# Attention output kept channel-major in a fused transformer-block kernel

## The reference

```python
x = L0_attn_x                       # (8, 1024, 256) float32
xn = layernorm(x)
q, k, v = split(xn @ W_attn + b_attn)      # 16 heads of 16 channels
q, k = rope(q), rope(k)                    # rotated by head index
att = softmax(causal(q @ k.T / 4))
s = (att @ v) @ W_proj + b_proj
h = silu(xn @ w_gate.T / 127) * (xn @ w_up.T / 127)      # hidden size 768
g = silu(h @ w_down.T / 127)
return x + s * g
```

## Time and profile before

| what | value |
|---|---|
| median of 3 runs | 1252.62 us (1247.04 to 1253.52) |
| the profiled execution's own time | 1248.4 us |
| its span, first to last instruction | 1246.7 us |
| mean granted TensorE clock | 0.992 |
| VectorE, ScalarE, GpSimd busy | 85%, 75%, 56% |

### The profile page before, as it was taken

The page is one execution under the profiler, slowest core; times in us unless marked ns, Lnnn a source line. Parts: engine busy times, 40 slices in busy tenths (PEclk is TensorE's granted clock), DMA queues, the critical chain, the costliest instruction groups (busy, mean ns, idle before and its releaser), DMA issues.

```text
span 1246.7 us, 28514 instructions
## 1 busy us (share of the span) xinstructions
PE 1180.0 (95%) x10044; PEld 507.0 (41%) x10044; DVE 1062.2 (85%) x3250; ACT 934.1 (75%) x1736; POOL 692.0 (56%) x858
## 2 busy tenths in 40 slices
...
DMA packets 55923, 73.10 MB, mean 59 GB/s; under 512 B 8382, under 2 KB 34372, under 8 KB 55780
## 3 DMA queue, kind: packets, MB, share of 16 engines
...
## 4 chain that ended last, share of the span: by engine, by line
PE 61%; DVE 18%; POOL 8%; ACT 7%; issue 5%; SPq 1%; DMA 1%; POOLq 0%; DVEq 0%; ACTq 0%
PE ring L838 28%; PE acc L829 13%; PE st L778 9%; PE ring L805 6%; DVE ring L1198 5%; DVE mx_a L1202 4%; ACT pexp L1037 2%; PE ring L911 2%; POOL hf L1526 2%; DVE ln L1233 1%; DVE ga L1266 1%; PE ring L947 1%; POOL hT L1535 1%; ACT yT L1044 1%; DVE ynT L1279 1%
## 5 line engine op out<-in xcount | busy, mean ns | idle before, releaser
L1037 ACT ACTIVATE pexp<-st 128x512 f32<-128x512 f32 x1152 | 623.3, 598 | 124.1 <-PE st L778 121.0
L1198 DVE CUSTOM_DVE_ANT_0 ring<-ring,tri 128x512 f32<-128x512 f32 (+3 forms) x1024 | 470.3, 523 | 29.3 <-PE ring L805 28.9
L1496 POOL TENSOR_SCALAR_AFFINE_SELECT pexp<-pexp 128x512 f32<-128x512 f32 x256 | 157.9, 635 | 407.1 <-ACT pexp L1037 407.1
L1202 DVE TENSOR_REDUCE mx_a<-ring 128x1 f32<-128x512 f32 x512 | 328.4, 684 | 17.1 <-PE ring L805 14.6
L829 PE MATMUL acc<-pexp,v_pad 128*17 128x512 f32 (+3 forms) x3072 | 303.7, 490 | 3.0 <-POOL pexp L1496 0.9
L805 PE MATMUL ring<-k_st,q_st 56*128 56x512 f16 (+4 forms) x1536 | 243.9, 326 | 14.9 <-POOL k_st L1617 3.7
L778 PE MATMUL st<-q_st,k_st 58*128 58x512 f16 (+3 forms) x1536 | 234.4, 331 | 6.3 <-ACT pexp L1037 3.8
L778 PEld LDWEIGHTS st<-q_st,k_st 58*128 58x128 f16 x1536 | 62.2, 93 | 267.8 <-ACT pexp L1037 172.1
L1526 POOL TENSOR_TENSOR hf<-ga,ups 128x512 f32<-128x512 f32 x96 | 122.4, 1275 | 40.6 <-issue 40.3
L829 PEld LDWEIGHTS acc<-pexp,v_pad 128*17 128x17 f32 x3072 | 61.3, 96 | 136.8 <-issue 121.2
L1535 POOL TENSOR_TENSOR hT<-hf,hT 128x512 f16<-128x512 f32 x96 | 111.2, 1158 | 3.4
...
## 6 DMA issues: line engine op xcount, KB each, us to landing
parts_scratch<-parts SPq DMA_DIRECT2D x32, 512.0 KB, 3.0
...
xo<-in_x SPq DMA_DIRECT2D x32, 256.0 KB, 3.0
out<-xo SPq DMA_DIRECT2D x32, 256.0 KB, 2.2
...
xn<-in_x SPq DMA_DIRECT2D x2, 512.0 KB, 6.0
```

The costliest lines, as they stand in the source:

```text
L1037: nc.scalar.activation(pexp[:, GH * (n % NSET) + j, :], st[:, (GH * n + j) % NST, :], ACT.Exp, scale=1.0 / (QK_SCALE * np.sqrt(D))).then_i ...
L1198: top_ = nc.vector.tensor_tensor_reduce(out=src, in0=src, in1=tri[:, CH - w:CH], scale=1.0, scalar=NEG, op0=ALU.add, op1=ALU.max, accum_ou ...
L1202: top_ = nc.vector.reduce_max(dst, src, AX.X)
L1496: nc.gpsimd.affine_select(out=t, in_=t, compare_op=ALU.is_ge, fill=0.0, base=0, pattern=[[0, GH], [1, P]], channel_multiplier=-1).then_inc ...
```

## The change

The result of attention stays channel-major, except in the last batch, where `YT` and `FT` stay. In the others `YS` (SyncE, 8 a batch) moves `yT` when a half of a group is done: one transfer stores the 4 rows of sums in memory, four put the heads' channels at their rows in `yp`. For a pair of groups (`kt`), `YG` loads the sums spread over 128 partitions, `YR` has VectorE take their reciprocal at once (128x64), `YB` stores them and `YC` spreads them with 8 transfers, a row to 16 partitions each, into `rb`. GpSimd then multiplies (`YN`), rounds (`YH`) and writes the remainder (`YL`), 4 times each a batch, 128x512. `FP` reads that. `MT` transposes once (128x64 to 64x128) and the maxima's 4 transfers a group lay 16 pieces of 256 bytes side by side. The parts are stored in memory as they are stacked (two transfers instead of one; three rows instead of two for each channel), so that a stack loads with 2 transfers, 4 for a group. The prologue's wide weights follow this order, with one more memset. The task table is new, with new lags. Removed and added lines, the core of it (the lines of arithmetic on counts and of the prologue's weights are left out):

```diff
 TASKS = {
-    0: [("UPG", 0, 0), ("DN", 1, 2), ("FT", 0)],
-    1: [("UPG", 0, 1), ("XC", 0)],
-    2: [("V", 0, 1), ("YT", 3, 1), ("FT", 1)],
-    3: [("DN", 1, 3), ("XC", 1)],
-    4: [("UPU", 0, 0), ("LNS", 0), ("LNS", 1)],
-    5: [("UPU", 0, 1), ("V", 1, 1), ("LNS", 2), ("LNS", 3)],
-    6: [("V", 1, 0), ("FP", 0), ("LNR",)],
-    7: [("MT", 1)],
-    8: [("UPG", 0, 2), ("LNA", 5), ("UPG", 0, 3), ("UPU", 0, 2), ("LNA", 2), ("YT", 0, 0)],
-    9: [("UPU", 0, 3), ("FT", 2)],
-    10: [("UPG", 0, 4)],
-    11: [("UPG", 0, 5), ("LNA", 4)],
-    12: [("LNA", 3), ("FP", 1)],
-    13: [("LNA", 6), ("UPU", 0, 4)],
-    14: [("UPU", 0, 5), ("YT", 1, 0), ("LNA", 0)],
-    15: [("LNA", 7), ("FT", 3), ("LNA", 1), ("FP", 2)],
-    16: [("UPG", 1, 0), ("MT", 2)],
-    17: [("TX", 0, 1), ("TX", 1, 1), ("UPG", 1, 1), ("DN", 0, 0)],
-    18: [("TX", 0, 0), ("DN", 0, 1), ("YT", 0, 1)],
-    19: [("TX", 1, 0), ("QK", 0, 1, 1)],
-    20: [("QK", 0, 1, 0), ("QK", 0, 0, 0), ("QK", 0, 0, 1), ("DN", 0, 2)],
-    21: [("DN", 0, 3)],
-    22: [("UPU", 1, 0)],
-    23: [("UPG", 1, 2)],
-    24: [("QK", 1, 1, 0), ("UPU", 1, 1)],
-    25: [("UPU", 1, 2), ("MT", 3), ("YT", 1, 1)],
-    26: [("UPG", 1, 3), ("UPG", 1, 4), ("UPU", 1, 3)],
-    27: [("UPU", 1, 4)],
-    28: [("UPG", 1, 5)],
-    29: [("FP", 3)],
-    30: [("UPU", 1, 5), ("YT", 2, 0)],
+    0: [("DN", 1, 2), ("XC", 0), ("YS", 3, 0)],
+    1: [("UPG", 0, 0), ("UPG", 0, 1)],
+    2: [("YS", 3, 1), ("V", 0, 1)],
+    3: [("XC", 1), ("YG", 1), ("DN", 1, 3)],
+    4: [("YR", 1), ("LNS", 0), ("UPU", 0, 0)],
+    5: [("LNS", 1), ("UPU", 0, 1), ("YB", 1), ("V", 1, 1), ("LNS", 2), ("LNS", 3)],
+    6: [("LNR",), ("YC", 1), ("YN", 1, 0), ("V", 1, 0)],
+    7: [("UPG", 0, 2), ("MT", 1), ("YS", 0, 0)],
+    8: [("YN", 1, 1), ("UPU", 0, 2)],
+    9: [("LNA", 5), ("UPG", 0, 3)],
+    10: [("UPU", 0, 3), ("LNA", 2), ("UPG", 0, 4), ("LNA", 1)],
+    12: [("FP", 0)],
+    13: [("UPU", 0, 4), ("LNA", 3), ("UPG", 0, 5)],
+    14: [("LNA", 6), ("YS", 0, 1), ("UPU", 0, 5)],
+    15: [("LNA", 0), ("LNA", 7), ("LNA", 4), ("FP", 1), ("FP", 2)],
+    16: [("YS", 1, 0), ("MT", 2), ("UPG", 1, 0)],
+    17: [("TX", 0, 1), ("TX", 0, 0), ("TX", 1, 1), ("UPG", 1, 1), ("DN", 0, 0)],
+    18: [("DN", 0, 1)],
+    19: [("YS", 1, 1), ("TX", 1, 0), ("QK", 0, 1, 1)],
+    20: [("QK", 0, 1, 0), ("QK", 0, 0, 1), ("YG", 0)],
+    21: [("QK", 0, 0, 0), ("DN", 0, 2), ("DN", 0, 3)],
+    22: [("YR", 0), ("UPU", 1, 0), ("UPU", 1, 1)],
+    23: [("FP", 3), ("UPG", 1, 2)],
+    24: [("YB", 0), ("QK", 1, 1, 0), ("YC", 0), ("UPU", 1, 2)],
+    25: [("MT", 3)],
+    26: [("YN", 0, 0), ("UPG", 1, 3), ("UPU", 1, 3), ("YS", 2, 0)],
+    27: [("UPG", 1, 4), ("YN", 0, 1)],
+    28: [("YS", 2, 1), ("UPU", 1, 4)],
+    29: [("UPG", 1, 5)],
+    30: [("UPU", 1, 5)],
     31: [("QK", 1, 1, 1)],
     32: [("QK", 1, 0, 0)],
-    33: [("DN", 1, 0)],
-    34: [("QK", 1, 0, 1), ("MT", 0), ("YT", 3, 0), ("YT", 2, 1)],
-    35: [("V", 0, 0), ("DN", 1, 1)],
+    33: [("DN", 1, 0), ("DN", 1, 1)],
+    34: [("QK", 1, 0, 1), ("MT", 0)],
+    35: [("V", 0, 0)],
 }
...
-    return task[0] in ("LNS", "LNR", "LNA", "TX", "QK") or task in (("V", 0, 0), ("MT", 0))
+    return task[0] in ("LNS", "LNR", "LNA", "TX", "QK") or task[0] == "YS" and task[1] < 3 \
+        or task[0] in PAIR and task[1] == 0 or task in (("V", 0, 0), ("MT", 0))
...
     "scalar": {"TX": 0, "QD": 0, "QK": 0, "UPG": 0, "UPU": 0, "V": 0, "DN": 0, "FT": 0, "FP": 0, "MT": 0},
-    "vector": {"TX": 0, "QK": 0, "UPG": 0, "DN": 0, "FT": 0, "YT": 0, "LNS": 1, "BP": 0},
-    "gpsimd": {"LNR": 0, "LNA": 1, "XC": 1, "UPU": 2, "HI": 3, "LO": 4, "FP": 2, "FP_G": 3, "FP_X": 4},
-    "sync": {"QK": 2, "MT": 1, "FP": 5},
+    "vector": {"TX": 0, "QK": 0, "UPG": 0, "DN": 0, "FT": 0, "YT": 0, "LNS": 0, "BP": 1, "YR": 0},
+    "gpsimd": {"LNR": 0, "LNA": 0, "XC": 1, "UPU": 2, "HI": 3, "LO": 4, "FP": 2, "FP_G": 2, "FP_X": 4, "YN": 0, "YH": 1, "YL": 2},
+    "sync": {"QK": 2, "MT": 0, "FP": 4, "YS": 0, "YG": 0, "YB": 0, "YC": 1},
...
+    sums_dram = nc.dram_tensor("sums_scratch", (2 * GH, T), fp32).ap()
+    inv_dram = nc.dram_tensor("inv_scratch", (2 * GH, T), fp32).ap()
+    parts_dram = nc.dram_tensor("parts_scratch", (2, 2, P, PARTS, T), fp16).ap()
...
+            sides = rows.rearrange("(p a d) r n -> a (d r) p n", a=2, d=D)
             for a in range(2):
-                for r, part in enumerate((0, 0, 1) if which == 0 else (0, 1, 0)):
-                    eng.dma_start(stack[SIDE * a + D * r:SIDE * a + D * r + D, g, :, :], parted[a, part])\
-                        .then_inc(stack_in[g], 16)
-        def rows_of_maxima(eng, g, heads):
-            for jj in heads:
-                row = SIDE * (jj // 2) + MAXROW
-                eng.dma_start(q_st[row:row + 2, g, jj % 2, :], mT[2 * jj:2 * jj + 2, :]).then_inc(mrow_in[g], 16)
+                eng.dma_start(stack[SIDE * a:SIDE * a + MROW, g, :, :], sides[a]).then_inc(stack_in[g], 16)
+        def rows_of_maxima(eng, g, sides):
+            for a in sides:
+                for part in range(2):
+                    row = SIDE * a + MAXROW + part
+                    first = 2 * TT * (2 * a + part)
+                    eng.dma_start(q_st[row:row + 1, g, :, :].rearrange("o p (t n) -> o (p t) n", t=TT),
+                                  mT[first:first + 2 * TT, :]).then_inc(mrow_in[g], 16)
...
+                low_at_row = LOW_ROW[which]
+                sp.dma_start(parts_dram[hf_, which, :, low_at_row - 1:low_at_row + 1, :], parts[:, which, :, :])\
+                    .then_inc(parts_out[which], 16)
...
+            def move_y(i, g, qc):
+                unit = pair_unit(i, g)
+                pair = pair_number(i + (g == 2), g // 2, qc)
+                wait(sp, acc_out, 2 * unit + qc + 1)
+                if g % 2 == 0:
+                    wait(sp, y_low, pair - 2)
+                stand(sp, sp_stand)
+                sp.dma_start(sums_dram[GH * (g % 2):GH * (g % 2) + GH, qc * CH:qc * CH + CH], yT[D:P:32, qc, :]).then_inc(y_moved[qc], 16)
+                for j in range(GH):
+                    row = 64 * (g % 2) + D * j
+                    sp.dma_start(yp[row:row + D, qc, :], yT[32 * j:32 * j + D, qc, :]).then_inc(y_moved[qc], 16)
+            def gather_sums(i, kt):
+                for qc in range(2):
+                    sp.wait_ge(y_moved[qc], 16 * (GH + 1) * pair_units(i, kt))
+                stand(sp, sp_stand)
+                sp.dma_start(ysum[:, :], sums_dram.rearrange("h (a r) -> (h a) r", r=4 * D)).then_inc(sums_in, 16)
+            def store_inverse(i, kt):
+                sp.wait_ge(inv_ready, pairs_before(i, kt) + 1)
+                stand(sp, sp_stand)
+                sp.dma_start(inv_dram.rearrange("h (a r) -> (h a) r", r=4 * D), yinv[:, :]).then_inc(inv_out, 16)
+            def spread_inverse(i, kt):
+                sp.wait_ge(inv_out, 16 * (pairs_before(i, kt) + 1))
+                wait(sp, y_scaled, 2 * pairs_before(i, kt))
+                stand(sp, sp_stand)
+                for h in range(2 * GH):
+                    sp.dma_start(rb[D * h:D * h + D, :, :].rearrange("p q n -> p (q n)"),
+                                 inv_dram[h:h + 1, :].broadcast_to([D, T])).then_inc(rb_in, 16)
...
+                    if turned(kind, t):
+                        wait_done(pe, kind, i, ("FT",) + t[1:])
+                    else:
+                        pe.wait_ge(y_low, pair_number(i, 1, tp // 2))
...
-                    for tt in range(TT):
-                        mm = nc.tensor.transpose(dst[0:2 * GH, :].bitcast(fp16)[:, tt * P:(tt + 1) * P],
-                                                 mx_p[:, tt, :, :].rearrange("p j a -> p (j a)"), ident16[:, :])
-                    mm.then_inc(ready, 1)
+                    nc.tensor.transpose(dst[0:2 * GH * TT, :].bitcast(fp16)[:, 0:P],
+                                        mx_p[:, :, :, :, :].rearrange("p a s j t -> p (a s j t)"), ident16[:, :])\
+                        .then_inc(ready, 1)
...
+                if i < B - 1 or g == 0:
+                    wait(act, y_moved[qc], 16 * (GH + 1) * (4 * i + g))
...
+                if t[0] == "YR":
+                    dve.wait_ge(sums_in, 16 * (pairs_before(i, t[1]) + 1))
+                    stand(dve, dve_stand)
+                    return nc.vector.reciprocal(yinv[:, :], ysum[:, :]).then_inc(inv_ready, 1)
...
+                if t[0] in ("YN", "YH", "YL"):
+                    _, kt, qc = t
+                    pair = pair_number(i, kt, qc)
+                    if t[0] == "YN":
+                        pool.wait_ge(y_moved[qc], 16 * (GH + 1) * pair_units(i, kt))
+                        pool.wait_ge(rb_in, 16 * 2 * GH * (pairs_before(i, kt) + 1))
+                        stand(pool, pool_stand)
+                        nc.gpsimd.tensor_tensor(yp[:, qc, :], yp[:, qc, :], rb[:, qc, :], ALU.mult).then_inc(y_scaled, 1)
+                    if t[0] == "YH":
+                        if kt == 0 and i > 0:
```

(38 more changed lines are left out.)

116 lines of the change are left out of this document (66 added, 50 removed).

## The result

The changed kernel takes 1266.72 us (median; 1262.84 to 1271.56), the kernel before, run beside it, 1250.02: a ratio of 1.0133, 95% interval 1.0106 to 1.0159. It is 1.3% slower, where 1228 and "faster" had been forecast. The profiled execution's span is 1266.8 us at a mean granted clock of 0.971; before it was 1246.7 at 0.992.

The account below looks back on a forecast made before the run. TensorE and GpSimd were both taken as full for 47 us from slot 5. Savings less stalls gave 14 (middle batches), 3.3, 3.8 and prologue 1.7: 22.8 off 1248.4, plus half of 4.2, 1228; forecast 1216 to 1236, 8-in-10 range 1200 to 1250.

Parts of the forecast that it names:

- Issued by 665.4 at the latest: SyncE's queue: YS 3,1 issued by then and YG likewise, landing by about 671, so YR costs nothing to 0.5 us.
- The list of what stands ahead of `YS` 3,1: SyncE's queue: two stacks at 1.8 us each, the next batch and two xo were counted ahead of that transfer.
- The two landings: Transfers of YS 3,1 and YG ahead of YR: taken to land 2.8 us after issue; 6.4 us was the slower possibility.
- the third rival: At YR: YS 3,1 and YG queue behind 3 MB and land late; 1278, or 1253 if one does; chance 0.13.
- one late transfer at 25 us: At YR: if only YS 3,1 or YG landed late, it would cost 25 us, giving 1253.
- the wait ahead of `YR`: Slot 4, sign of error: VectorE idle on a transfer there, or YR on the chain, would show late sums.
- a fixed 2.0 us: Transfers ahead of YR: by this cited cost both landings take 4.1 us together and YR is not late.
- a stand of 2 to 4 us before `TX` or at the masks of slots 11 to 14: TensorE would idle there on GpSimd; the sum counted some 3.5 us a middle batch.
- `DN` 0,0's wait for the gate product: Behind slot 17's TX, VectorE waits for GpSimd's FP 1 product: 0.7 us more, partly covered by the ring's banks.
- The stand of slot 28: TensorE waits for GpSimd before the values, after the second half's added YN work: 1.5 us a batch.
- The sum's 5.7 us a batch: Stalls given back per middle batch on GpSimd's work: 3.5 + 0.7 at slot 17 and 1.5 at slot 28.
- TensorE's saving: YT, FT and MT transposes shed: 7.3 us a middle batch, 52.8 us together, before stalls are taken off.

Follow-up runs that it names:

- y_small: The changed kernel with GpSimd's YN, YH and YL on 16 of 512 columns, most attention output left at zero: 1250.92 us, 1.0016 times the kernel before.
- both: The changed kernel with group 3's stacks loaded in slot 4 and YN, YH, YL on 16 of 512 columns: 1233.37 us, 0.9858.
- maxima_only: The kernel before with only the change's stacks and maxima (one MT transpose, 2 loads a stack); old table, YT and FT kept: 1243.38 us, 0.9945.
- stack_late: The changed kernel with group 3's stacks loaded in slot 4, behind YS 3,1, instead of slot 2: 1249.06 us, 0.9991.
- early_norm: stack_late with the next x loaded 12 slots earlier, layer norm and UPU 0,0 and 0,1 earlier, YN 1,0 and FP 2 moved: 1282.96 us, 1.0236.
- maxima_early: maxima_only with the next x loaded early, LNS in slots 0 to 3, LNR in 4 and two LNA moved: 1271.81 us, 1.0166.

## Why the prediction was wrong, step by step

**SyncE's queue: the step that failed first.** "Issued by 665.4 at the latest" is 10.7 us behind slot 0 (654.74); measured are 15.45 (687.03 - 671.58). The list of what stands ahead of `YS` 3,1 named two stacks, the next batch and two `xo`, and left out `YS` 3,0, whose five transfers are in the same queue: 677.12 to 680.94, 3.8 us. The rest is issuing that was slower than the earlier trace rows: 1.36 us for the two `xo`, and 1.77 for a pair of stack loads that takes 0.83 elsewhere. Large transfers were moving at the time; that they are the reason isn't shown. The two landings, over which the text argued at length, were 2.6 us each, a little below the 2.8 taken. So the third rival was the right one ("the sums come late", given 0.13), its mechanism wrong in one word: it had the transfers land late, and they were issued late. It priced one late transfer at 25 us; the waits are 20.6 us in seven batches, and 17.7 us went with one line. That the measured time lies inside its range (1250 to 1280) is partly luck: 17.7 us on top of the forecast's 1228 give 1246, and the rest comes from the next steps. The text had itself named the wait ahead of `YR` as what would prove it wrong.

The Trainium skill's page "DMA: Bandwidth & Descriptors", section "Anatomy of one DMA", was cited for a fixed 2.0 us, which it states for GpSimd's path; these transfers go out by SyncE's queue. The two landings give 5.2 us together, and 4.1 by an estimate from the page's figure: the difference of 1.1 is the smaller part of the 2.88 us at `YR`, and here the measurement decides.

**GpSimd: right in kind and nearly in place.** Forecast: a stand of 2 to 4 us before `TX` or at the masks of slots 11 to 14; found: 2.01 and 0.70 us at the masks of slots 11 and 10, and 0.4 before `TX` (0.9 for its weight load). `DN` 0,0's wait for the gate product was foreseen at 0.7 us and is 1.7 a batch on VectorE (10.3 us in 6). The stand of slot 28 was forecast at 1.5 us, and only 0.3 is seen, on a weight load. The sum's 5.7 us a batch (35.7 us with the first batch) are more than twice the 15.8 us of y_small. GpSimd's busy time was forecast at 97 to 98 us a batch and is 96.0. `YR` takes 0.55 us, not 0.3.

**TensorE's saving: the term that was mis-sized.** 7.3 us a batch were taken as arriving in full, less the stalls. In the run both, which is free of the two costs, TensorE's busy time falls by 6.7 us where the clock stays up (143.4 to 136.75), and those batches are 3.1 us shorter (145.45 to 142.3); on average of the six, with the lower clock in four, it is 1.6 (143.9). maxima_only, at full clock throughout, gives 0.4 of 0.8. So about half arrives, and less than a quarter once the clock has taken its part. The other half stands as idle time: TensorE is idle for 5.6 us of such a batch in the run both and for 2.0 before. The pauses that are new are 1.32 us in slot 6, for a maximum on VectorE, and 0.97, 0.30 and 0.33 in slot 25, the first for VectorE's work on the query and key parts. What the new transfers cost beyond the late sums was not tested by itself: every run on the changed table has them, and weight loads of `scores` wait 17.1 us in after (16.9 in both) for the transfers of maxima, 0.9 before. The forecast had read that GpSimd is full from slot 5 to 17 and VectorE holds slots 0 to 5, and counted on TensorE all the same. The runs show both limits from either side: 4 us of VectorE's work moved into slots 0 to 3 (with `LNR` and two `LNA` behind it) cost 3.9 a batch; two statistics of 1 us each moved back by one slot cost 5 by GpSimd's queue. Between them, the table has next to no slack. The end of the execution, where `YT` and `FT` stay and GpSimd has less to do, did get shorter, by 6.0 us.

**How the steps add up.** Without the stalls that it charged to GpSimd's new work (35.7 us) the forecast would have been 1192 us; the run both, which has hardly any of that work and no late sums, takes 1233. So the saving was taken 41 us too large. The stalls were taken 20 us too large (35.7 against 15.8), and the late sums, 17.7 us, were left out. 41 less 20 plus 18 is the miss of 39 us. The too large saving is thus the biggest error, and half of it was hidden by the too large stalls. Without the late sums the kernel would have been no faster than before (stack_late, 0.9991), so they made "no change" into "slower".

**The clock: not in the sum.** Every stall was counted at its length. In the six middle batches TensorE is busy for 837.1 us in after and 827.6 in the run both, with the same matmuls, and at the lower clock for 44 against 20 us. (Over the whole execution the difference is 15.7 us; 6.2 of that lie before the first batch's `TX`, where the start-up's own time at the lower clock, 24 and 10 us here, differs from run to run.) Late sums and GpSimd's work differ here. Taking the late sums away halves the time at the lower clock (44 to 20 us in the six batches, after to stack_late, and y_small to both); taking GpSimd's work away leaves it (44 in y_small, 20 in the run both). These are single executions, but the mean clocks of all agree: at 0.978 after took 1262.8 us and y_small 1250.2 and 1248.2, so 13 to 15 of its 15.8 us aren't the clock's. Within y_small's ten executions the time goes from 1246.6 us at 0.981 to 1258.3 at 0.972, about 1.3 us for a thousandth. The median executions of after and stack_late are 0.006 to 0.007 apart; by that, an estimate, some 8 of the 17.7 us came by the clock and the rest by the waits themselves. What decides whether a pause is followed by the lower clock stays open. So does how early_norm's 34 us above stack_late divide: beside the early layer norm, of which maxima_early shows 28, its weight loads wait up to 5.8 us for the maxima's transfers (37.5 us in all, 17.0 in stack_late).
